# The seam between two attention stages: ones of the second tile asked for later, two queues for the first copies, w2 behind four maxima

## The reference

```python
x = _layernorm(x + _L0_attn_ref(x, ...))            # stage A
x = _layernorm(x + _L0_xattn_ref(x, ctx, ctx, ...)) # stage B
x = _layernorm(x + _L0_ffn_ref(x, ...))             # stage C
```

```python
s1 = einsum('bshe,bthe->bhst', q1, k1) / 4
s2 = einsum('bshe,bthe->bhst', q2, k2) / 4
attn = softmax(s1) - gain * softmax(s2)
o = einsum('bhst,bthe->bshe', attn, vp)
```

## Time and profile before

| what | value |
|---|---|
| median of 3 runs | 1487.13 us (1484.43 to 1487.58) |
| profiled execution | 1487.18 us, span 1485.2 us |
| time outside the span | 1.98 us |
| mean granted TensorE clock | 0.996 |
| PE busy | 1452.2 us, 98% of the span |
| DVE, ACT, POOL busy | 1135.8, 791.8, 392.3 us |

### The profile page before, as it was taken

One profiled execution on the slowest core, in us unless ns is written; L12 is line 12 of the kernel. 1 busy time (PEld: TensorE's weight loads), 2 busy tenths in 40 slices (PEclk: granted clock), 3 DMA queues, 4 the chain that ended last, 5 costly groups with the idle time before them and its releaser, 6 DMA issues.

```text
span 1485.2 us, 28345 instructions
## 1 busy us (share of the span) xinstructions
PE 1452.2 (98%) x10885; PEld 1029.9 (69%) x10885; DVE 1135.8 (76%) x2251; ACT 791.8 (53%) x1091; POOL 392.3 (26%) x432
## 2 busy tenths in 40 slices
PE   8999999999999999999999999999999999999998
PEld 5444444434566666666567888988889898888987
DVE  6445544377899999999977888788786878788786
ACT  5887888865778778878763422313222231222221
POOL 1000101223655777666454410000000000000001
PEclk9999999999999999999999999999999999999999
DMA  7766667456657657666552201010010101110001
GB/s 153 154 111 123 115 118 128 92 105 109 99 91 110 99 89 113 95 96 99 88 167 71 79 15 37 22 29 21 23 30 15 43 16 29 29 29 16 21 22 29
DMA packets 90235, 108.88 MB, mean 73 GB/s; under 512 B 18400, under 2 KB 58668, under 8 KB 90100
## 3 DMA queue, kind: packets, MB, share of 16 engines
q1 hardware_dynamic: 89768, 106.67, 38.3%
q10 hardware_dynamic: 332, 0.39, 0.1%
HBM read 26.07 MB, written 4.19 MB: 20 GB/s over the span
## 4 chain that ended last, share of the span: by engine, by line
PE 78%; DVE 10%; issue 3%; SPq 3%; ACT 3%; POOL 1%; DMA 1%; POOLq 0%; DVEq 0%; ACTq 0%
PE ps L109 76%; DVE NM L1710 3%; SPq L119 3%; ACT PX L1650 1%; ACT H L708 1%; PE ps L1474 1%; PE ps L1466 1%; DVE PR L1704 0%; POOL X L1902 0%; DVE X L1697 0%; DVE GH L2608 0%; DMA TA<-TX 0%; DVE GH L2610 0%; DVE GF L2604 0%; PE ps L1397 0%
## 5 line engine op out<-in xcount | busy, mean ns | idle before, releaser
L1710 DVE TENSOR_REDUCE NM<-ps 128x4 f32<-128x1024 f32 x256 | 308.2, 1221 | 32.2 <-PE ps L109 29.8
L1650 ACT ACTIVATE PX<-ps 128x1024 f32<-128x1024 f32 x256 | 262.2, 1024 | 98.8 <-PE ps L109 96.1
L708 ACT ACTIVATE H<-ps 128x1024 f32<-128x1024 f32 x240 | 230.0, 1033 | 43.9 <-PE ps L109 41.8
L2379 ACT ACTIVATE GF<-ps,cols 128x512 f32<-128x512 f32 x128 | 87.2, 687 | 220.4 <-PE ps L109 204.8
L109 PE MATMUL ps<-XC,W_sw_w 128*128 128x512 f32 x768 | 187.2, 393 | 0.0
L109 PEld LDWEIGHTS ps<-XC,W_sw_w 128*128 128x128 f32 x768 | 140.1, 188 | 27.6
L2730 POOL TENSOR_SCALAR RSc<-AGc 128x4 f32<-128x4 f32 x23 | 6.0, 259 | 571.1 <-DVE AGc L2494 571.1
L109 PE MATMUL ps<-PX,VT 128*32 128x256 f32 x2048 | 137.9, 387 | 2.9 <-DVE X L1697 1.3
L2610 DVE TENSOR_TENSOR GH<-GF,GH 128x512 fp32r<-128x512 f32 x192 | 133.9, 698 | 6.6
L2374 ACT ACTIVATE GF<-ps 128x512 f32<-128x512 f32 x64 | 38.1, 596 | 183.7 <-PE ps L109 183.7
L109 PE MATMUL ps<-KT,QT 48*128 48x512 f32 x512 | 128.1, 498 | 3.4 <-DMA QT<-XSb 1.7
(11 more groups left out here) (266 smaller groups left out, 2460.2 us busy)
## 6 DMA issues: line engine op xcount, KB each, us to landing
KT<-KS SPq DMA_DIRECT2D x128, 192.0 KB, 4.7
ST<-QS SPq DMA_DIRECT2D x254, 96.0 KB, 2.8
QT<-XSb SPq DMA_DIRECT2D x128, 96.0 KB, 4.2
XR<-TT SPq DMA_DIRECT2D x352, 32.0 KB, 1.9
XT<-in_xT_dram SPq DMA_DIRECT2D x8, 512.0 KB, 4.2
raw_a<-in_x_dram SPq DMA_DIRECT2D x8, 512.0 KB, 4.2
CR<-in_ctxT_dram SPq DMA_DIRECT2D x8, 512.0 KB, 4.0
out_dram<-X SPq DMA_DIRECT2D x7, 512.0 KB, 2.9
```

Source lines behind the costliest of these rows:

```text
L708: e.activation(H1[s % 8][:, :, :], PP[s % 3][:, :, :], ACT.Tanh, bias=0.0 if s > 15 else b1c[:, half:half + 1], scale=1.0).then_inc(act_th, 1)
L1650: e.activation(PX[s % 3][:, :, :, :], PP[2][:, :, :].rearrange("p g (c q) -> p g c q", c=2), ACT.Exp, bias=0.0, scale=0.25).then_inc(act_e ...
L1710: e.tensor_reduce(NM[u % 2][:, qc, :, :, i], PP[qc][:, :, :].rearrange("p g (m k) -> p g m k", m=2), AX.X, ALU.max, negate=True).then_inc( ...
L2379: e.activation(g[:, :], o, f, bias=cols[:, col:col + 1], scale=1.0).then_inc(act_g, 1)
```

## The change

It changes no arithmetic. Five pieces:

1. `ones_rows(1)`, the ones of the second key tile, goes from step -6 to step 5 on SP. It counts on another semaphore (`d_w` in place of `d_ones`), and only scores of block 1 and later wait for it.
2. Of `put_maxima(0)` SP issues only the first half. ACT issues the second, right behind its copy to `NR`.
3. `load(1, 3)` goes from SP (step 2) to ACT, behind that half: `last_load`, four DMAs.
4. `LAST_W2` goes from -13 to -11: the last `w2` group stands behind `maxima(3)` instead of `maxima(1)`, and ACT's eviction of it behind the `KS` copy. The three fillers of step -11 go.
5. `prep_v(0, 0)` goes from step -11 to -8.

```diff
-LAST_W2 = -13
+LAST_W2 = -11
...
-BUSY = {-11: 3, -10: 1, -9: 1, -8: 1, -7: 1, -6: 1, -5: 1, -4: 2, -3: 1, -2: 1}
+BUSY = {-10: 1, -9: 1, -8: 1, -7: 1, -6: 1, -5: 1, -4: 2, -3: 1, -2: 1}
...
-        return {-11: (0, 0), -7: (0, 1), -3: (0, 2), -1: (0, 3)}.get(s)
+        return {-8: (0, 0), -7: (0, 1), -3: (0, 2), -1: (0, 3)}.get(s)
...
-                    f32(ones[:, :, :]).rearrange("r m t -> r (m t)").unsqueeze(1).to_broadcast([4, 4, 1024]), d_ones)
+                    f32(ones[:, :, :]).rearrange("r m t -> r (m t)").unsqueeze(1).to_broadcast([4, 4, 1024]), d_w if i else d_ones)
...
-            for g in range(2):
+            for g in range(2 if u else 1):
                 dma(e, f32(q[64 * g + 48:64 * g + 52, :, b, :]), f32(NR[u % 2][16 * g:16 * g + 16, :]), d_mr[u % 2])
...
-                if B is not None:
+                if B is not None and (B, i) != (1, 3):
                     load(B, i)
-            for i, at in enumerate((-16, -6)):
+            for i, at in enumerate((-16, 5)):
...
-            w.wait_ge(d_ones, 80)
+            w.wait_ge(d_ones, 48)
+            if B:
+                w.wait_ge(d_w, 80)
...
+        def last_load():
+            w.wait_ge(pool_ks, 4)
+            w.wait_ge(dve_ks, 4)
+            w.wait_ge(pool_xs, 6)
+            after(w, "w2")
+            for g in range(2):
+                h = 6 + g
+                dma(e, f32(KT[1][64 * g:64 * g + 48, 3, :, :]).rearrange("r m t -> r (m t)"),
+                    f32(KS[16 * h:16 * h + 16, 1, :, :, :]).rearrange("d l m t -> d (l m t)"), d_ld[1][3])
+                dma(e, f32(QT[1][64 * g:64 * g + 48, 3, :, :]).rearrange("r b t -> r (b t)"), f32(XS[16 * h:16 * h + 16, 1, :, :]), d_ld[1][3])
...
                 e.activation(NR[u % 2][:, :], low7[0:32, :], ACT.Copy).then_inc(act_nr, 1)
+                if u == 0:
+                    w.wait_ge(act_nr, 1)
+                    dma(e, f32(QT[0][112:116, :, 0, :]), f32(NR[0][16:32, :]), d_mr[0])
+                    last_load()
```

## The result

| | before | after |
|---|---|---|
| median, same chip | 1487.13 us (1483.56 to 1490.67, 13 runs) | 1492.22 us (1488.9 to 1495.65, 13 runs) |
| ratio, 95% interval | | 1.0032 [1.0021, 1.0044] |
| profiled execution, its span | 1487.18, 1485.2 us | 1495.65, 1493.8 us |
| mean granted clock | 0.996 | 0.991 |

The change makes the kernel slower by 0.32%, some 4.8 us, and the time lies outside the range of the prediction. The profiled execution of the change is the slowest of its 13 runs, 3.4 us over their median; that of before lies at its median. The page of the profile after already gives a direction. TensorE has three matmuls fewer than in the earlier trace rows and is 3.9 us busier: the same work ran slower.

A forecast was written before the change was run, and what follows sets the result against it. TensorE, with work in hand for 98% of the span, was taken as the bound. Terms -2.3 - 1.5 - 0.2 + 1.9 + 0.8 = -1.3 against 1487.18 gave 1485.9 us, range 1482.8 to 1489.0.

The forecast's parts named there:

- clock term: Behind TensorE's new idle ahead of prep_v(0, 3): half the price of a low-clock stretch, +0.8 us (0 to 1.5).
- ScalarE asks: Five DMA issues between NR and SQ on ScalarE delay the first scores by 1.9 us; clock behind the idle adds 0.8.
- if the clock falls somewhere else that no row of before tells of: A named way for the prediction to fail, anywhere in the kernel; no size given.
- w2: Last w2 group behind four maxima: VectorE's idle of 1.06 before the third maximum partly returns, gain 0.2 us (0 to 1.06).
- hold: ScalarE's five issues ahead of SQ make the first scores late by 1.9 us (cases -0.2, 1.9 or 5.3).
- stall: TensorE's idle at step 8, 1.66 for load(1, 3) and 0.64 for the maxima, goes: -2.3 us.
- slow stretch: Low clock from the scores of step 8 to 12 goes: -1.5 us, taken between 0.86 and 2.39.
- Five at 1.3: ScalarE's five issues beside SP's take 1.3 us each, 6.5 in all.
- Rival A: ScalarE gets its five issues through at SP's pace, 4.4 us, with no idle: 1483.3 us; chance 0.30.
- Rival B: ScalarE's issues take 1.98 each and the clock falls: +2.8 us, or 1490.5 with one of 2.54; chance 0.12.
- Rival C: Transfers decide, so moving issues gives nothing and the step 8 stall returns in full: 1487.2 us, less 0.2; chance 0.12.
- The ones: Second tile's ones at step 5 on SP, two issues of 2.23 us, behind the second maxima: cost nothing.

The follow-up runs named there:

- ones_act: Kernel before with the ones at step 5 and the second half of the first maxima and load(1, 3) on ScalarE, w2 as before: 1.0028, 1491.96 us.
- act_only: Kernel before with only the second half of the first maxima and load(1, 3) moved to ScalarE: 1.0030 against before, 1491.27 us.
- fill: Whole change plus seven fillers ahead of prep_v(0, 3) and the three of step -11 back: 0.9996 against the kernel before, 1486.58 us.
- sp_later: Whole change, with SP's load(1, 1) held until ScalarE has copied prep_v(0, 2): 0.9984 against the kernel before, 1485.11 us.
- ones_only: Kernel before with only the second tile's ones at step 5 in place of -6, with their semaphore: 0.9965 against before, 1482.75 us.
- half_ones: Kernel before with the ones at step 5 and only the second half of the first maxima on ScalarE: 0.9967 against before, 1483.09 us.
- spread: half_ones with load(1, 3) on ScalarE too, one issue behind each exp of steps 0 to 3: 0.9968 against the kernel before, 1483.37 us.
- w2_only: Kernel before with only the last w2 group behind four maxima, its three fillers gone and prep_v(0, 0) at step -8: 1.0016 against before, 1489.76 us.
- no_act: The change without its ScalarE part, first maxima and load(1, 3) whole on SP: 0.9972 against the kernel before, 1483.32 us.
- fill_v: Whole change plus seven fillers ahead of prep_v(0, 3), those of step -11 left out: 0.9991 against the kernel before, 1486.63 us.
- after_again: The whole change run once more, unaltered: 1.0035 against the kernel before, 1491.68 us.

## Why the prediction was wrong

**The step that failed is the clock term of "ScalarE asks": "I put half the price of such a stretch here too: 0.5 x 1.5 = 0.8 (0 to 1.5)".** The direction was in the text, the size was not. I took the price from the one stretch of the trace, 6.8 us long, of which steps 8 to 12 had given 1.5. Behind the new idle the stretch lasted 13.65 us in both traces of the change and in `ones_act`, and 10.2 in `act_only`, and it cost 5.1 us in the traces (1.50 from `NR` to the first scores and 3.60 in steps 0 to 4). The upper bound of 1.5 was too low by more than a factor of three: it assumed that a second stretch could be no longer than the first, and no dearer for its length. It was both: 5.1 / 13.65 = 0.37 for each us, against 1.5 / 6.9 = 0.22. In steps 8 to 12 TensorE has a wait of 1.23 for VectorE at full clock, ahead of the product `C,OT` (at 368.60 in the change), which is not there in the slow stretch of before, so part of that stretch was hidden.

**A second term was missing.** The sum has no clock cost for the moved `w2` group, and its slow stretch took another 1.44 in the trace. The prediction names such a case only as a way to fail ("if the clock falls somewhere else that no row of before tells of"). Together the two are the 6.6 of the traces and the 5.4 of the runs.

**The rest of the sum was nearly right, in part by luck.** The fillers take the clock out and leave the rest, and `fill`'s column reads: `w2` +0.10 (forecast -0.2), hold +2.10 (1.9), stall -2.50 (-2.3), slow stretch -1.50 (-1.5). The forecast without its clock term was -2.1; `fill` gives -1.80 in the trace. By the runs it gives 0.9996 [0.9980, 1.0011], -0.6 us with -1.8 inside the interval. By the ratios the hold is 3.6 rather than 2.1; the intervals are too wide to say that it is more. The 1.5 for the slow stretch was a choice between 0.86 and 2.39, and nothing in the working made it right. Inside the hold small errors cancel. From the first issue to ScalarE's release `fill` has 6.17 (forecast 6.5), from there to `prep_v(0, 3)` 1.08 (0.92), and from there to the first scores 1.71 (1.55). That last figure came from 2.18 less a wait "of some 0.6", but the wait in the trace of before is 0.37.

**ScalarE's issues.** Five at 1.3 were to take 6.5; they took 6.35, 6.32 and 6.17. The rows at 13.4 gave the right total, but not the single issues: these took 0.75, 0.67, 1.72, 1.81 and 1.18. Rival A, in which ScalarE gets its issues through at SP's pace, is refuted for the change. Its arithmetic (4.4) holds once SP is silent (`sp_later`: 4.44).

**Rival B came, by half of its mechanism.** "The hold is longer than the stall was, and the clock falls behind it" was priced with issues of 1.98 each. The issues did not take that, the hold was the forecast one, and the clock fell all the same. Its deciding point, 8.3 us for the five, was wrong, because it asked for long issues first and a falling clock behind them. An idle of 2.33 was enough for the fall. The forecast itself had 2.5 of idle; it was 3.09 and 3.07.

**Rival C, and the rule of the Trainium skill** ("DMA: Bandwidth & Descriptors", "Issuing engines are not separate DMA queues": issuing from several engines saves only issuing time, usually small). By the prediction's reading the rule would have no gain from any of this. The measurement parts it in two. What stood ahead on one queue was worth 0.35% here: `ones_only` sends the same bytes, those of the ones some 21 us later, and takes the stall away. But the second issuing engine gave nothing over that (`half_ones` 0.9967, `spread` 0.9968, `ones_only` 0.9965). The stall went in every kernel with the ones moved, so the transfers of `load(1, 3)` and of the maxima did not decide. Those of the ones may have. The prediction read the DMA share of 0.23 as engines with room and put the delay down to the issue. But 0.23 is near a quarter of the 16 engines, and the low rate ends with the slow issue: windows of half a microsecond show, in the trace of before, 16 to 33 GB/s from 333.0 to 336.5, none from 336.5 to 337.0 and 90 to 106 from 337.5 to 339.5, and the issue ends at 336.56. In `act_only` both queues' slow issues end at 336.9 and the rate of 33 GB/s at 337.0; in `w2_only` it is 340.46 and 340.5. So the issue seems to be held until the ones have been moved; no run shows it by itself.

**The ones.** Forecast at no cost, and the rows agree: in `ones_only` the second unit's maxima leave at 349.34, with `load(1, 3)` still ahead of them on SP, and the scores of step 8 do not wait. What I missed is that this piece carries the whole gain by itself. The prediction named the 2.54 and put it down to the ones. It did not work out what is left of the stall once the pair takes 1.42 in place of 3.33. From the pair's first issue to the second unit's maxima SP's queue takes 351.01 - 333.22 = 17.79 before and 349.34 - 334.01 = 15.33 in `ones_only`: 2.46 less, and the stall was 2.30.

**w2.** Forecast -0.2. With the clock at full, `NR` starts 0.10 earlier in `no_act` (12.27 against 12.37 behind the first maxima). VectorE's third maximum does follow the second without the 1.06 of the earlier trace rows, here in the trace of the change, but the gain ends there, since TensorE's third and fourth maxima then wait for the reductions:

```profile
323.93 3.49 DVE L1728 TENSOR_REDUCE NM<-ps 128x4 f32<-128x1024 f32 x3
```

TensorE's small idles of 0.20 and 0.63 are new there, and in four of six profiles with `w2` moved and no fillers of step -11 (the change twice, `w2_only`, `sp_later`; not `no_act`, `fill_v`) the group ran at half clock, 3.1 to 3.6 for 1.92. It did not in `fill`, which has those fillers, nor in any of the profiles with `w2` in its old place. This was not foreseen.

**Right as told:** no idle before the maxima and scores of step 8, and full clock from step 8 to 12. The second maxima were to leave at about 348 and be in time: in `fill` they leave at 348.55, in the change, where their `NR` is copied only at 358.37 behind the slowed steps, at 358.75. The scores of step 8 start 6.45 and 6.46 later and wait in neither. The first scores, forecast at 342, came at 341.55 in `fill`, at 348.16 in the change and at 345.12 in `after_again`, whose first maxima come when before's do; in `after_again` low clock makes nearly all of the part over 342, and in the change 2.94 more came in from ahead.

**The better version.** `ones_only`, one number in a table of steps and one semaphore, runs at 0.9965 [0.9952, 0.9978]: 5.0 us faster than before by the medians, and faster than the change by 0.67% (1.0032 - 0.9965).

**Open.** What sets whether a low stretch comes, and whether it lasts 3.4, 6.8, 10.2 or 13.65 us; I have lengths and no rule. Whether an issue behind the ones waits for their transfer. Whether the stretch in the `w2` group comes from the idles of 0.20 and 0.63 or from the missing fillers was not separated, and two profiles with those idles lack it. And the hold's own price is 2.1 to 2.7 in traces, 3.6 by the runs.

## What to carry to other kernels

When an issue is slow, ask first what stands ahead of it on its queue: putting off two DMAs that nothing needed yet gave everything that five moved to another engine were to give. Before DMAs are given to a computing engine, look at which of its results TensorE waits for next; the same four issues cost 0.6% ahead of such a copy and nothing inside the exps a few microseconds later. Price a new TensorE idle of 2 to 3 us in an otherwise dense stream not by its length but by the low-clock stretch behind it, which may come or not, and do not take the longest stretch that you have seen as the bound; if the idle can't be avoided, a few fillers in it are a cheap insurance.

## What the runs showed of the hardware

- **The clock after an idle.** In every profile with an idle of 2.3 us or more in the seam a stretch at half clock began during it or within about 5 us of its start: before (1.66 and 0.64 with 0.5 of work between: 6.8 us), the change (3.09 and 3.07: 13.65 twice), `ones_act` (2.33: 13.65), `act_only` (3.56: 10.2), `w2_only` (2.75 and 0.32: 10.2). In the seven others (`sp_later`, `fill`, `fill_v`, `no_act`, `ones_only`, `half_ones`, `spread`) the longest idle in the seam is 1.24, and the only stretch is that of the `w2` group in `sp_later`. In the change TensorE was busy for 12.17 of the 13.70 us at the low level, without a break from 345.13 on, so dense work does not bring the clock back at once.
- **The length of the idle alone does not decide.** Near 20 us all 13 profiles run the same unedited work, with one wait for `ST<-QS`. A stretch at half clock began in the wait itself or within 2.1 us of its end in eight of them, with waits of 1.22 (`no_act`), 1.45, 1.54, 1.94, 1.94, 1.95, 2.21 and 3.13, and in five it did not, with waits of 1.51, 1.55, 1.69, 1.84 and 1.86 (`spread`). The stretches lasted 3.4 us, and 6.8 in the change and in `ones_act`. This may be part of why executions of one kernel differ.
- **Two queues issuing together are slower.** The same five issues on ScalarE: 4.44 alone, 5.92 to 6.35 beside SP, and 7.14 where the ones stand ahead on SP as well (`act_only`).
- **An issue behind the ones is slow, on either queue.** Behind `KT<-ones_b` the second `QT<-NR` takes 2.54, or the pair 4.33 (`w2_only`), and 1.42 for the pair without it. In `act_only` SP's and ScalarE's `KT<-KS` take 2.54 and 2.46 side by side, although the ones went out on SP's queue.
- **ScalarE issues while it computes.** In `spread` an issue started 0.00 to 0.09 after the exp ahead of it had started, and took 0.57 to 0.90 of the exp's 1.03.
